# Spreading queries and keys by 32-row products, and reordering the work around them, in causal and full attention

## The reference

```
x = x + diff_attention(layernorm(x))                        # stage A1
x = x + moe_gelu(layernorm(x))                              # F1
x = x + causal_attention(layernorm(x))                      # A2
x = x + moe_gelu(layernorm(x))                              # F2
x = x + single_head_attention(layernorm(x))                 # A3
x = x + block(layernorm(x))                                 # A4, F3
x = x + recurrent_block(layernorm(x))                       # RI, RR, RM
x = x + block(layernorm(x))                                 # A5, F4

def causal_attention(x):          # 16 heads of 8
    q, k, v = x @ Wq.T, x @ Wk.T, x @ Wv.T
    p = softmax(where(key <= query, q @ k.T / sqrt(8), min))
    return (p @ v) @ Wo.T
def block(X):                     # full attention, then a mixture of experts
    h = rmsnorm(X, norm1_w);  q, k, v = h @ wq, h @ wk, h @ wv
    X = X + (softmax(q @ k.T / sqrt(8)) @ v) @ wo
    h2 = rmsnorm(X, norm2_w);  logits = h2 @ router_w      # top 2 of 8 experts
    return X + shared(h2) + experts(h2, logits)
```

## Time and profile before

| | |
|---|---|
| median of 3 runs | 2730.9 us (2723.22 to 2736.89) |
| profiled execution | 2730.92 us, its span 2729.2 us |
| PE matmul | 2255.9 us busy, 83% |
| DVE | 1791.8 us, 66% |
| ACT | 1568.8 us, 57% |
| POOL | 1325.0 us, 49% |
| TensorE clock granted, mean | 0.925 of full |

### The profile page before, as it was taken

One profiled execution on the slowest core, in us unless ns is written; L12 is line 12 of the kernel. 1 busy time (PEld: TensorE's weight loads), 2 busy tenths in 40 slices (PEclk: granted clock), 3 DMA queues, 4 the chain that ended last, 5 costly groups with the idle time before them and its releaser, 6 DMA issues. The chain is left out here.

```text
span 2729.2 us, 65546 instructions
## 1 busy us (share of the span) xinstructions
PE 2255.9 (83%) x19720; PEld 1641.4 (60%) x19720; DVE 1791.8 (66%) x4959; ACT 1568.8 (57%) x3495; POOL 1325.0 (49%) x2493
## 2 busy tenths in 40 slices
PE   5999997999498888995978888896567778888895
PEld 3666665699365555895845555595233445555695
DVE  5667766444577775444767878566677567877566
ACT  2555554367376664575648788344255258777344
POOL 3557665455256775453234555454311334555463
PEclk9999999899599998997979999898877879999897
DMA  2000000322200003123000000224000000000224
GB/s 58 1 5 11 10 11 9 103 63 71 68 2 11 15 14 92 49 72 99 0 5 4 15 13 16 80 81 114 9 0 0 6 5 6 14 14 14 84 84 137
DMA packets 132260, 100.01 MB, mean 37 GB/s; under 512 B 23159, under 2 KB 119941, under 8 KB 132032
## 3 DMA queue, kind: packets, MB, share of 16 engines
q1 hardware_dynamic: 97088, 51.95, 7.1%
q0 software_dynamic: 18304, 36.88, 4.0%
q10 hardware_dynamic: 16640, 8.39, 1.2%
HBM read 58.22 MB, written 40.76 MB: 36 GB/s over the span
## 5 line engine op out<-in xcount | busy, mean ns | idle before, releaser
L1150 ACT ACTIVATE A_Pm<-A_t 128x768 f32<-128x768 f32 (+1 forms) x512 | 469.1, 916 | 209.4 <-PE A_t L1571 205.6
L339 POOL DMA_INDIRECT ybuf<-F_yo,F_idx x284 | 297.2, 1046 | 264.1 <-DVE F_yo L537 133.4
L1563 PE MATMUL A_s<-A_K,A_Q 32*128 32x256 f32 (+1 forms) x2640 | 326.5, 340 | 82.9 <-DVE A_mx L1351 60.2
L1351 DVE TENSOR_REDUCE A_mx<-A_s 128x4 f32<-128x1024 f32 x264 | 321.5, 1218 | 85.6 <-PE A_s L1563 78.3
L1035 POOL TENSOR_SCALAR_AFFINE_SELECT A_Pm<-A_Pm 128x256 f32<-128x256 f32 x512 | 216.9, 447 | 228.8 <-ACT A_Pm L1150 226.1
L192 POOL DMA_INDIRECT xbuf<-xs,dst x256 | 264.6, 1034 | 125.9 <-issue 60.5
L1598 PE MATMUL A_ot<-A_Pm,A_V 128*32 128x256 f32 (+3 forms) x3640 | 299.5, 394 | 25.6 <-POOL A_Pm L1035 16.6
L1563 PEld LDWEIGHTS A_s<-A_K,A_Q 32*128 32x128 f32 x2640 | 193.3, 188 | 199.9 <-issue 103.1
L1571 PE MATMUL A_t<-A_Q,A_K 32*128 32x256 f32 (+1 forms) x2560 | 306.3, 333 | 0.0
L673 PE MATMUL F_hb<-F_xT,F_wt 128*128 128x128 f32 x2272 | 303.9, 277 | 2.3 <-DVE F_wt L547 1.2
L673 PEld LDWEIGHTS F_hb<-F_xT,F_wt 128*128 128x128 f32 x2272 | 275.7, 191 | 5.6 <-ACT F_xT L378 1.9
(11 more groups left out here) (434 smaller groups left out, 5118.7 us busy)
## 6 DMA issues: line engine op xcount, KB each, us to landing
F_xr<-xbuf SPq DMA_DIRECT2D x284, 68.0 KB, 1.8
xs<-ybuf ACTq DMA_DIRECT2D x16, 512.0 KB, 11.3
xs<-ybuf SPq DMA_DIRECT2D x16, 512.0 KB, 10.0
ybuf<-F_yo,F_idx POOLq DMA_INDIRECT x284
xbuf<-xs,dst POOLq DMA_INDIRECT x256, 2.3
F_WA<-in_L_ffn_ew SPq DMA_DIRECT2D x2, 2048.0 KB, 9.4
F_WA<-in_L_ffn_ew SPq DMA_DIRECT2D x16, 256.0 KB, 5.5
F_WA<-in_L_ffn_e_gate SPq DMA_DIRECT2D x2, 1024.0 KB, 5.6
```

The costliest lines, as they stand in the source:

```text
L339: pool.indirect_dma_start(out=YBUF[:, :], out_offset=bass.IndirectOffsetOnAxis(ap=idx[n][:, h:h + 1], axis=0), in_=yo[r][:, h, :], in_offs ...
L1150: act.activation(Pm[r][:, j:j + 2, :], tbank[:, :].rearrange("p (j k) -> p j k", j=2)[:, :, 0:PW], ACT.Exp, scale=SCALE).then_inc(t_free, 1)
L1351: last = dve.reduce_max(tops.rearrange("p t j -> p j t"), sbank[:, :].rearrange("p (j t k) -> p j t k", j=2, t=TPS), AX)
L1563: last = pe.matmul(sbank[:, k * 512 + o:k * 512 + o + nk], Q1[q][r, c + t * P:c + (t + 1) * P], K1[q][r, c:c + nk], start=not masked, stop ...
```

## The change

In the causal and full stages:

- `project` gives way to `spread`: for two groups at once, queries and keys of each in one bank, by products of 32 rows with 128 columns out and 256 columns in. The two groups of a step sit in different row tiles and different banks. The -1 rows of the keys come from a third product (`minus` with `ones_r`), so ACT's bias and the column `colc` go. `Q1` and `K1` become views of one tile `QK`.
- The maxima are turned by a one-pass product (float32r) with an identity in that type in place of a transpose; POOL writes their high part straight into `padm`, one operation less.
- x (in g1) and the routing's rows (in g0 and g3 of p = 1) are turned in the free half of the products' bank, within `turn_back`, and ACT takes them within `context`. T, RT0 and RT1 leave the shared banks' order. `xT` and `O` are doubled, and ACT waits for the context of one sequence earlier.
- The dense projection and its low part move from the end of a sequence to g2, with V; QK3 moves to g1.
- DVE's slots: normalization to (0, 1), statistics to (1, 1), context to (2, 0), `next_stat` (causal) to the end of the sequence. POOL: other `SENDS`, `next_root` and `root` in other rounds, and the second normalization of the full stages comes from ACT to POOL.

The diff is cut to its core; the differential stage A1 keeps its order, in branches of its own that are not shown.

```diff
...
     G["spread"] = {n: ctx.enter_context(nc.sbuf_tensor(f"spread_{n}", [P, k], F32R)) for n, k in (("one", 528), ("q", 512), ("k", 512))}
+    G["minus"], G["ones_r"], G["identr"] = [ctx.enter_context(nc.sbuf_tensor(n, [P, k], F32R)) for n, k in (("minus", P), ("ones_r", SEQ), ("identr", P))]
...
                 dve.memset(G["spread"][n][:, :].bitcast(F32), 0.0)
+            dve.memset(G["minus"][:, :].bitcast(F32), 0.0)
+            dve.memset(G["ones_r"][:, :].bitcast(F32), 1.0)
...
+            dve.memset(heads(G["minus"][:, :].bitcast(F32))[:, :, 24:26], -1.0 / 32)
+            dve.tensor_copy(G["identr"][:, :], ident[:, :])
             dve.wait_ge(unit_set, 2)
...
     split = not diff
+    xTs = [sb(f"xT{k}", [P, SEQ]) for k in range(2)] if split else [sb("xT", [P, SEQ])] * 2
     QT = F32R if split else F32
...
-    K1 = [sb(f"K1_{k}", [P, NTL * SEQ], QT) for k in range(2)]
+    QK = [sb(f"QK_{k}", [P, NTL, 2, SEQ], QT) for k in range(2)]
+    Q1, K1 = [[a[:, :, n, :] for a in QK] for n in range(2)]
...
+    padm = [sb(f"padm{k}", [P, TPS, QUAD, GR], QT) for k in range(2)]
+    Os = [sb(f"O{k}", [P, TPS, NMAP, OV]) for k in range(2)] if split else [sb("O", [P, TPS, NMAP, OV])] * 2
     rec = sb("rec", [P, TPS, NMAP])
     ctx = sb("ctx", [P, TPS, VW])
...
         before = ["T", "D", "QK0", "QK1", "QK2", "QK3", "V", "T1", "D1"]
-        order = ["QK0", "QK1", "QK2", "V", "QK3", "T", "ctxT", "y", "D"]
-        routed_order = ["RT0", "QK0", "QK1", "QK2", "V", "QK3", "T", "RT1", "ctxT", "y", "D"]
+        order = routed_order = ["QK0", "QK1", "QK2", "QK3", "V", "D", "ctxT", "y"]
...
+    SENDS = (1, 1, 0, 2) if full else (0, 2, 1, 1)
+    turned_bank = obank[:, SEQ:2 * SEQ]
     sent, R = w["sent"], w["next"]
     RSRC = X if R == "gelu" else Y
...

             def maxima(n, r):
                 pool.wait_ge(s_free, n * 2 + 3)
-                pool.wait_ge(mt_full, n)
-                pool.tensor_tensor(mh[:, :, :], mx[r][:, :, :], nil8[:, :, :], ALU.add).then_inc(m_high, 1)
+                if n > 0:
+                    pool.wait_ge(mt_full, n)
+                pool.tensor_tensor(padm[r][:, :, :, MROW], mx[r][:, :, :], nil8[:, :, :], ALU.add).then_inc(m_high, 1)
                 pool.wait_ge(m_high, n + 1)
-                pool.tensor_tensor(padm[r][:, :, :, MROW], mh[:, :, :].bitcast(F32), nil8[:, :, :], ALU.add)
-                pool.tensor_tensor(padm[r][:, :, :, MROW + 1], mx[r][:, :, :], mh[:, :, :].bitcast(F32), ALU.subtract).then_inc(m_split, 1)
+                pool.tensor_tensor(padm[r][:, :, :, MROW + 1], mx[r][:, :, :], padm[r][:, :, :, MROW].bitcast(F32), ALU.subtract).then_inc(m_split, 1)
+
+            def second_norm(b):
+                pool.wait_ge(xhat_ready, b + 1)
+                pool.tensor_tensor(xn[:, :, :], YS[:, b + S0, :, :], rs3[:, :].unsqueeze(2).to_broadcast([P, TPS, D]), ALU.mult).then_inc(xn_ready, 1)

             if split:
-                pool.wait_ge(s_free, 3)
-                pool.tensor_tensor(mh[:, :, :], mx[0][:, :, :], nil8[:, :, :], ALU.add).then_inc(m_high, 1)
-                pool.wait_ge(m_high, 1)
-                pool.tensor_tensor(padm[0][:, :, :, MROW], mh[:, :, :].bitcast(F32), nil8[:, :, :], ALU.add)
-                pool.tensor_tensor(padm[0][:, :, :, MROW + 1], mx[0][:, :, :], mh[:, :, :].bitcast(F32), ALU.subtract).then_inc(m_split, 1)
+                maxima(0, 0)
                 root(2)
...
                     else:
+                        if g == 1 and full:
+                            second_norm(b + 2)
                         for k in range(SENDS[g]):
                             if n >= 4 * NQ + FIRST_SEND and sends < EARLY * 2 * TPB:
                                 send(sends)
@@ -1090,9 +1095,9 @@
                             add_context(b - 1)
                             if 3 <= b < EARLY * TPB // TPS + 3:
                                 first_copy(b - 3)
-                        elif g == 1:
+                        if g == (1 if full else 0):
                             next_root(b)
-                        elif g == 3 and b + 3 < NSEQ + 2:
+                        elif g == 2 and b + 3 < NSEQ + 2:
                             root(b + 3)
                     if masked:
...
-                c = slice(k // 2 * 512, (k // 2 + 1) * 512)
+                if split:
+                    take(m, QK[q][:, k, :, :], misc[:, :].rearrange("p (a n) -> p a n", a=2))
+                    return
...
-            def context(n, g, k):
+            def context(n, g, k, p, turned=None):
                 act.wait_ge(ob_full, n + 1)
-                if g == 0:
-                    act.wait_ge(norm_chain, k * NNORM + 3) if diff else act.wait_ge(ctx_ready, k + 1)
+                if g == 0 and diff:
+                    act.wait_ge(norm_chain, k * NNORM + 3)
+                elif g == 0 and (not isinstance(k, int) or k > 0):
+                    act.wait_ge(ctx_ready, k)
+                O = Os[1 - p if g == 3 else p]
                 for s in range(NS):
                     last = act.activation(O[:, :, g * QUAD:(g + 1) * QUAD, :].rearrange("p t (h s) d -> p s t h d", s=NS)[:, s],
                                           obank[:, s * SEQ:(s + 1) * SEQ].rearrange("p (t h d) -> p t h d", t=TPS, d=VG)[:, :, :, 0:OV],
                                           ACT.Identity)
+                if turned is not None:
+                    dst, scale = turned
+                    last = act.activation(dst, turned_bank, ACT.Identity, scale=scale)
                 last.then_inc(o_free, 1)
...
@@ -1196,12 +1215,6 @@
                     last = act.activation(squares_next[:, t, :], YS[:, b + S0 - 2, t, :], ACT.Square, accum_out=ssq_next[:, t:t + 1])
                 last.then_inc(mv_next_ready, 1)

-            def second_norm(b):
-                act.wait_ge(xhat_ready, b + 1)
-                for t in range(TPS):
-                    last = act.activation(xn[:, t, :], YS[:, b + S0, t, :], ACT.Identity, scale=rs3[:, t:t + 1])
-                last.then_inc(xn_ready, 1)
...
-                        elif full and g == 2:
-                            second_norm(b + 2)
                         if g == 3:
                             ctx_turned(use(i, p, "ctxT"), bank_of(i, p, "ctxT"))
                         exp(n, 1, g % 2)
-                        context(n, (g + 3) % NQ, b)
-                        if starts and p == 1 and g == 0 and not diff:
-                            route_turned(i - 1, 0, use(i, p, "RT0"), bank_of(i, p, "RT0"))
-                        if g == 0:
-                            if split:
+                        if split:
+                            turned = None
+                            if g == 1:
+                                turned = xTs[p][:, :], insc[:, :] if full else 1.0
+                            elif starts and p == 1 and g in (0, 3):
+                                turned = route_taken(i - 1, 0 if g == 0 else 1)
+                            context(n, (g + 3) % NQ, b, p, turned)
+                            if g == 0:
                                 quads(use(i, p, "QK0"), 0, 1 - p, bank_of(i, p, "QK0"))
-                            quads(use(i, p, "QK1"), 1, 1 - p, bank_of(i, p, "QK1"))
-                        elif g == 1:
-                            if starts and p == 1 and diff:
-                                route_turned(i - 1, 0, use(i, p, "RT0"), bank_of(i, p, "RT0"))
-                            quads(use(i, p, "QK2"), 2, 1 - p, bank_of(i, p, "QK2"))
-                            values(use(i, p, "V"), 1 - p, bank_of(i, p, "V"))
-                            if starts and p == 1:
-                                route_copied(i - 1, 0)
-                        elif g == 2:
-                            quads(use(i, p, "QK3"), 3, 1 - p, bank_of(i, p, "QK3"))
-                            x_turned(use(i, p, "T"), bank_of(i, p, "T"))
-                            if starts and p == 1 and split:
-                                route_turned(i - 1, 1, use(i, p, "RT1"), bank_of(i, p, "RT1"))
+                                quads(use(i, p, "QK1"), 1, 1 - p, bank_of(i, p, "QK1"))
+                            elif g == 1:
+                                quads(use(i, p, "QK2"), 2, 1 - p, bank_of(i, p, "QK2"))
+                                quads(use(i, p, "QK3"), 3, 1 - p, bank_of(i, p, "QK3"))
+                                if starts and p == 1:
+                                    route_copied(i - 1, 0)
+                            elif g == 2:
...
-                steps = {(0, 1): (next_stat,), (1, 0): (reciprocals,), (1, 1): (context, norm), (2, 1): (stat,)}
-                if full:
-                    del steps[0, 1]
+                steps = {(0, 1): (norm,), (1, 0): (reciprocals,), (1, 1): (stat,), (2, 0): (context,)}
...
+                if masked:
+                    next_stat(0, lead["T"] + 1)
...
+                            if split and (g, half_) == (2, 1):
```

(61 more changed lines are left out.)

166 lines of the change are left out of this document (87 added, 79 removed).

## The result

The changed kernel takes 2836.8 us (median of 5 runs, 2832.6 to 2848.2) where the kernel before takes 2730.4 beside it: a ratio of 1.039, 95% interval [1.037, 1.041], 3.9% slower. The forecast was 2720 and its range ended at 2748.

The account below looks back on a forecast made before the run. Bound taken: PE, ACT and DVE waiting for each other in the attention loops, no engine filling the time. Full stages -13.6 us and causal +3, in all -10.6, gave 2720; own forecast 2706 to 2735, whole range 2680 to 2748.

Parts of the forecast that it names:

- the ring: In the attention loops PE, ACT and DVE wait for each other; an undisturbed causal half takes 1.94 us.
- the one that reached 2768: Rival, chance 0.10: the 32-row products run one by one, 1.2 us a spreading, 48 us in all.
- Spreading: Query and key spreading: ten 32-row products in five concurrent pairs take 0.6 us, two banks before 1.12; no gain by itself.
- the whole pause of 0.21: Weight-load idle between 128-row mask products and 32-row scores; 0.1 us a switch counted, the whole costing 0.2 more a causal sequence.
- Maxima: Turning the maxima: one POOL operation of 0.2 us less and shorter turns; 0.05 us taken where it counts.
- Rows in the products' bank, dense projection in g2: Second sequence of a pair: no shared-bank wait, -0.2 us full, -0.43 causal; moved projection -0.2 full, +0.1 causal.
- just hidden: Causal halves with a spreading: two more tiling switches, PE needing 1.7 to 1.95 us of the 1.94.
- Sum: Full pair -1.0 us, two full stages -13.6, causal stage +3, in all -10.6: 2720 us.
- The relaxed ring: Rival, chance 0.28: doubled O adds slack, each of 24 pairs loses 2 us more: 2672, or 2696 with half.
- POOL's sends: Rival, chance 0.12: late maskings reach g3 in the causal stage, 2 to 3 us more a pair: 2736 to 2744.
- POOL's late weighing: Causal g1: two sends between maskings delay weighing to 6.0 us after g1A's scores; g2B's scores at 7.24, before 7.0.
- The second normalization: Full stages: moved from ACT (0.7 us) to POOL, 0.74 by the nearest row, bounds 0.4 and 1.5; effect 0.

Follow-up runs that it names:

- e8: The changed kernel, unchanged, run again on the chip where the kernel before takes 2732 us: ratio 1.038 to before, attention loops 1027 us.
- e7: The kernel before, unchanged, run again with a trace: 2732 us, ratio 1.000, attention loops 918 us.
- e9: The changed kernel with spreading by ten 128-row products per pair of banks and maxima turned by two f32 transposes: ratio 1.008 to before, loops 937 us.
- e15: The changed kernel with before's sixteen 128-row products a sequence, ACT's bias and f32 transposes of the maxima: ratio 0.998 to before, loops 923 us.
- e1: The changed kernel with its spreading by 128-row products again, one-pass turn of the maxima kept: ratio 1.015 to before, loops 953 us.
- e2: The changed kernel with the maxima turned by f32 transposes again, 32-row spreading kept: ratio 1.014 to before, loops 951 us.
- e10: The kernel before with only the one-pass turn of the maxima added: ratio 1.007 to before, loops 934 us.
- e3: The changed kernel plus four unread one-pass 128-row products ahead of each turn of the maxima: ratio 1.050 to before, loops 1092 us.
- e16: The changed kernel plus one unread f32 product of query with key weights ahead of each turn of the maxima: ratio 1.026 to before, loops 994 us.
- e17: The changed kernel plus one unread f32 product of the identity with itself ahead of each turn of the maxima: ratio 1.026 to before, loops 993 us.
- e18: The changed kernel, unchanged, run once more on the chip used for the first follow-ups: ratio 1.040 to before, loops 1028 us.

## Why the prediction was wrong

**The step that failed** is the cost of PE work taken out. "The halves concerned end on maxima or ACT, so it wins nothing by itself" was right as to the ring, and from it I took that less work on PE can't lose. The sum has no term for the clock: it goes on at before's, 0.98 in the earlier trace rows, which I used only as a column. The runs showed 0.71 to 0.88 in its place, and loops 109 us longer on one chip (1027 less 918, e8 and e7). Of that, 90 us are the two edits together, 32-row products for the 128-row spreading and one-pass products for the maxima's transposes (e8 less e9); the other 19 are e9's, most of them the four 128-row products a sequence that e15 does without (937 less 923, across chips). Each edit alone costs about 15 us beside e9 (e1 or e2 less e9, across chips; 0.7% by the ratios): the losses don't add, they come together. How the clock is set, and so why these edits lose it, stays open. No rival of mine ended there; the one that reached 2768 did so by another mechanism.

**Spreading.** Right that the pairs run together, wrong in what they save. Five pairs of products behind a turn back, the scores after them held up only by DVE:

```profile
1517.51 0.44 PE L1638 MATMUL A_ot<-ident,A_OT 128*128 128x128 f32 x2
1517.88 0.38 PE L1569 MATMUL A_misc<-A_high,spread_q 32*128 32x256 f32 x2
1518.10 0.28 PE L1569 MATMUL A_misc<-A_low,spread_one 32*128 32x256 f32 x2
...
1518.46 0.28 PE L1569 MATMUL A_misc<-ones_r,minus 32*128 32x256 f32 x2
1518.90 0.38 PE L1595 MATMUL A_s<-A_QK 32*128 32x256 f32 x2 [0.16 <-DVE A_mx L1374]
```

and the same place of the kernel before:

```profile
904.52 0.44 PE L1606 MATMUL A_ot<-ident,A_OT 128*128 128x128 f32 x2
904.72 0.36 PE L1539 MATMUL A_misc<-A_high,spread_k 128*128 128x256 f32 x1
904.92 0.28 PE L1540 MATMUL A_misc<-A_low,spread_one 128*128 128x256 f32 x1
```

Pairs start 0.12 us apart, but the first step is 0.22: 0.70 us for the five, forecast 0.6. The step is no switch of tiling, since the 128-row products have it too (904.72 to 904.92). The switch stands ahead of the first pair: 0.37 us behind the start of the turn back, where the 128-row product starts 0.20 behind it. That is 0.17 and not the 0.1 that I took, nearer to the whole pause of 0.21 in the earlier trace rows. Back to the mask's 128-row products, in A2, it is 0.21 from the last pair (805.81 to 806.02), for the usual 0.12. The products don't run one by one.

**Maxima.** Forecast 0.05 us a half where it counts; measured nothing as an edit alone (e10), and a lower clock.

**Rows in the products' bank, dense projection in g2.** Right in form. `low` waits for `high`, and the maxima of g3A follow it:

```profile
1511.34 0.69 DVE L1318 TENSOR_TENSOR A_low<-A_misc,A_high 128x512 fp32r<-128x512 f32 x1 [1.09 <-ACT A_high L1135]
1511.95 1.22 DVE L1374 TENSOR_REDUCE A_mx<-A_s 128x4 f32<-128x1024 f32 x1
```

A plain full sequence took 16.95 us at the full clock (roundings of the high part at 1510.71 and 1527.66) for 17.2: -0.25, forecast -0.2. A full pair took 38.5 to 38.6, forecast 38.4.

A plain causal sequence took 17.8 (778.97 to 796.75) for 17.1, +0.7 where I had +0.1. Two terms are too low in it. In e15, which has the moved work without the new spreading, it takes 17.45 (789.95 to 807.40): +0.35 is the moved work, as much as the half with the next layer's statistics has lost by itself (2.37 us for 2.01). The other 0.33 is the spreading, with either form of the turn (e2 has 17.78 too): I had it "just hidden". It sits in the halves behind a spreading, 2.20 and 2.23 us for e15's 1.96 and 2.02: ACT waits for the last of the ten products, takes both banks in a row, and its exponential comes later:

```profile
787.76 1.29 ACT L1128 ACTIVATE A_QK<-A_misc 128x512 fp32r<-128x512 f32 x2 [0.18 <-PE A_misc L1569]
788.94 0.81 ACT L1158 ACTIVATE A_Pm<-A_t 128x768 f32<-128x768 f32 x1
```

**Sum.** At a full clock the moved work nearly does in the causal stage what I forecast, and less in the full ones. The windows of e15: a causal pair with sends, then a full pair:

```profile
845.12:885.62 40.50, 34.11 (x401) 22.78 (x401) 31.51 (x99) 25.87 (x54) 26.04 (x65) 1.00 0.04 13
```

```profile
1609.85:1649.06 39.21, 31.64 (x369) 20.97 (x369) 32.11 (x72) 29.72 (x60) 22.08 (x48) 1.00 0.04 14
```

The causal pair has 40.5 for 39.95 before and a forecast of 40.4. The full pair keeps 0.2 us of the 0.8 that the changed kernel gains at the full clock. Where the other 0.6 come from takes both edits: e2, with the 32-row spreading and the transposes, has 39.23 and 39.03 us, e1, with the one-pass turn and 128 rows, 39.43:

```profile
1581.57:1620.80 39.23, 30.82 (x377) 19.63 (x377) 32.24 (x72) 29.55 (x60) 22.24 (x48) 1.00 0.04 14
2434.73:2473.76 39.03, 31.13 (x377) 19.70 (x377) 32.10 (x72) 29.44 (x60) 22.24 (x48) 1.00 0.04 14
```

```profile
1542.15:1581.58 39.43, 32.43 (x377) 22.60 (x377) 31.97 (x72) 29.79 (x61) 20.18 (x46) 1.00 0.04 12
```

So 38.5 is had only in the one version that can't keep the clock. By whole loops e15's A4 and A5 have 304.7 and 304.4 us for 304.5 and 307.0, -2.4 us where I forecast -13.6, and A2 314.3 for 306.7, +7.6 for +3. These hold the clock too (A2 at 0.97 for 0.99: three sequences below the full clock, 23.45 and twice 21.09 us for 20.61, cost 3.8 of the 7.6) and compare two chips.

**The relaxed ring**, 0.28 by my chances, wanted 2 us more from every pair; at the full clock the pairs gained 0.8 to 0.9 us (full) and lost 0.5 (causal, e15). It falls.

**POOL's sends**, 0.12 by my chances, cost no 2 to 3 us a pair beyond the sum: 40.5 us is what the sum had. They do bind more than before. In a causal pair of e15 (885.62 to 926.04) PE waits for POOL's masking three times, 2.3 us in all, for 0.7 us in the pair of before; the longest:

```profile
902.65 0.86 PE L1626 MATMUL A_ot<-A_Pm,A_V 128*32 128x256 f32 x16 [1.03 <-POOL A_Pm L1040]
```

That is in form what the sum has as POOL's late weighing. The second normalization takes POOL 0.61 us, for 0.74 taken.

## What to carry to other kernels

Read the clock column before costing a removal on TensorE. Where the clock is near full in a loop, the matmul work that seems to be free to take out may be holding it: look at it as a resource, and try an edit that lightens PE beside a copy with useless PE work added. If the copy is faster, it was the clock; if it is slower, nothing follows (e3), and the clock column has to be read. Undo edits singly and together: beside e9 each of these two costs about 0.7%, and both cost 3.0%.

## What the runs showed of the hardware

- The granted clock fell to half again and again while PE was busy for 353 of 380 us; the busy share gave no sign of it (before: 269 of 306, clock 0.99). At half clock the busy share rises, since the same products last longer.
- With four useless f32 products a sequence a causal loop ran in 328 and 327 us for 365 and 380, clock 0.95 for 0.77 and 0.71, whatever the data (e16 and e17, for e18 and e8). Sixteen one-pass products in the same places: 369 us, clock 0.83.
- A 128x128 one-pass f32 product was no shorter than an f32 transpose (301 and 300 ns), and its weight load longer, 188 ns for 140.
- 32-row f32 products in two row tiles and two banks start in pairs 0.12 us apart, as 128-row ones do singly. Going from 128-row to 32-row products cost 0.17 us (0.37 for 0.20, start to start), and going back 0.09 (0.21 for 0.12).
- One chip ran the feed-forward stages 5 to 7% faster than two others (F1 280 us for 300, F2 353 for 370), with the sums of the attention loops alike to some 10 us.
